# Sixteen copies of the residual spread over the first stage, and the biases and second expert's weights loaded after the first transposition

## The chip, the cores and the metric

The kernel runs on one core of a Trainium2 chip. The metric is the device time of one launch in microseconds (us), as the median of several runs. The core has a matrix engine (TensorE, PE in the profile), three engines for elementwise work (VectorE or DVE, ScalarE or ACT, GpSimd or POOL) and SyncE (SP), which here only issues DMA transfers. Each engine works its own list of instructions in order and waits on semaphores that others raise. The rows of SP's DMA issues stand under SPq.

## The reference

`x` is 128 x 64 x 256 in fp32, that is 8192 rows (tokens) of 256. A modulated linear layer makes a hidden row of each token, a mixture of eight experts is applied to it, and the result is added to `x`:

```python
scale = 1.0 / np.sqrt(np.float32(256)); ys = cond * scale                # per batch entry
d   = rsqrt(einsum('bi,io->bo', ys * ys, weight * weight) + EPS)
hid = einsum('bsi,io->bso', x * ys[:, None, :], weight) * d[:, None, :]
logits = hid @ wr.T; vals, idx = top_k(logits, 2); gating = softmax(only those two)
# each expert takes at most cap = 2560 tokens, in order of their number
xg = hid_pad[dispatch]                                                   # (8, cap, 256)
h  = gelu(einsum('ecd,edf->ecf', xg, w1) + b1[:, None, :])               # 256 -> 1024
y  = einsum('ecf,efd->ecd', h, w2) + b2[:, None, :]                      # 1024 -> 256
out = x + segment_sum(y * gate, dispatch)                                # back to the tokens
```

## The kernel before, in words

**First stage.** The tokens are worked in 16 groups (`GROUPS`) of 512. SP loads a group of the transposed `x` into one of four buffers (`load_x`, `X_RING` is 4), POOL scales it (line 336), PE multiplies it by the modulation weights (line 464), ACT and DVE scale the product (lines 672 and 810), PE turns it back to rows and computes the logits (lines 477 and 479), ACT copies the rows to `rows` (line 657). For every two groups (a set, `SETS` is 8) DVE picks the two best experts and a slot in their lists, POOL writes the gates, and SP stores the set in `hidden` in DRAM (`store_rows`, line 301). DVE and PE also build the lists of tokens; the one-hot matrices that this takes lie in the memory of `b2_sb` and `h_raw`, which is free for its own data only when all groups are listed (semaphore `listed`). The weights of the first expert are loaded at the start and split into a high and a low part during this stage (lines 648 and 779).

**Second stage.** Each expert's list is worked in blocks of 384 tokens. POOL gathers a block's rows from `hidden` with three indirect DMAs (`gather`, line 391), PE transposes them (line 537) and raises `t_done`, ACT makes the high part `xt_hi` (line 690), DVE the low part `xt_lo` (line 928). A block has eight chunks of 128 hidden units: `first_product` (lines 547 to 549), two GELU activations on ACT (line 701), a subtraction on DVE (line 969), `second_product` (lines 559 to 561). PE runs three first products ahead: the first product of chunk f waits for the GELU of chunk f-3 (`bank_read`). After the first product of chunk 6 PE transposes the rows of the next block. At the end of a block DVE adds `b2` (line 994) and multiplies by the gates, and POOL adds the rows into `out` in DRAM by an indirect DMA with addition (line 404). Before the first of these additions POOL waits for `out_written`, the count of the copies.

**Weights of the next expert.** `load_weights` is two DMAs of 1 MB each into `w_raw`. They may start when DVE has made all eight low parts of the expert before (`w_lo_done`). In the first two blocks of an expert, after the GELUs of chunks 2, 3, 4 and 5, ACT copies one piece of the next expert's weights each (`split_piece`, line 648), and DVE subtracts it (line 779). Before the first piece ACT waits for both DMAs (`w_loaded`), and its later GELUs stand behind this wait.

**Copies of x.** The output starts as a copy of `x`: `copy_x(g)` moves 512 KB from DRAM to DRAM in one DMA (line 280). Before the change SP issues the 16 copies in a row when everything is listed, behind the load of `b2`.

Of the kernel before, what the change touches and what calls it, by code (L numbers as in the profile page):

```python
# [16 lines left out]
P = 128  # L17
# [11 lines left out]
GROUPS = T // ROWS  # L29
GB = ROWS // S  # L30
PAIR = 2
SETS = GROUPS // PAIR
TS = PAIR * TILES
X_RING = 4
# [35 lines left out]
def build(nc, x, x_t, cond_t, w, wr_t, w1, b1_t, w2, b2, ident, tri, expert_low, slot_base, middle_ids, lanes,  # L70
# [9 lines left out]
    with ExitStack() as ctx:  # L80
        def sb(name, shape, dt=F32):
            return ctx.enter_context(nc.sbuf_tensor("sb_" + name, shape, dt))

        def sem(name):
            return ctx.enter_context(nc.semaphore(name))
# [16 lines left out]
        b2_sb = sb("b2", [P, E * D])  # L102
# [80 lines left out]
        b2_in = sem("b2_in")  # L183
# [32 lines left out]
        listed = sem("listed")  # L216
# [12 lines left out]
        t_done = sem("t_done")  # L229
# [37 lines left out]
        def all_blocks(eng, less=0):  # L267

            at = less * (E + 1) + E
            return eng.value_load(plan[0:1, at:at + 1], min_val=16 * (E * LEAST - less * LAG)) // 16  # L270
# [3 lines left out]
        @block.sync  # L274
        def _(sp):
            def load_x(g):
                sp.dma_start(x_in[g % X_RING][:, :, :], x_cols[g, :, :, :]).then_inc(x_loaded[g % X_RING], 16)

            def copy_x(g):
                sp.dma_start(out_copy[g, :, :], x_copy[g, :, :]).then_inc(out_written, 16)  # L280

            def load_weights(e):
                sp.dma_start(w_raw[:, 0:WCOLS].rearrange("p (k f) -> p k f", k=KC),
                             w1_rows[e, :, :, :]).then_inc(w_loaded, 16)
                sp.dma_start(w_raw[:, WCOLS:2 * WCOLS].rearrange("p (c d) -> p c d", c=FC),
                             w2_rows[e, :, :, :]).then_inc(w_loaded, 16)

            load_x(0)
            sp.dma_start(w_sb[:, :, :], w.rearrange("(k p) o -> p k o", p=P)).then_inc(w_in, 16)
            for g in range(1, X_RING):  # L290
                load_x(g)
            sp.wait_ge(set_dve, 1)
            for s in range(SUBS):
                sp.dma_start(hidden[T + s * P:T + (s + 1) * P, :], empty_sb[:, :]).then_inc(pad_zero, 16)
                sp.dma_start(out[T + s * P:T + (s + 1) * P, :], empty_sb[:, 0:D]).then_inc(out_written, 16)
            load_weights(0)

            def store_rows(s):

                sp.wait_ge(rows_ready, s + 1)  # L300
                sp.dma_start(hidden[s * TS * P:(s + 1) * TS * P, :].rearrange("(j p) c -> p j c", p=P),
                             rows[s % ROW_RING][:, :, :]).then_inc(rows_stored[s % ROW_RING], 16)

            for g in range(X_RING, GROUPS):
                sp.wait_ge(m_done, KC * (g - X_RING + 1))
                load_x(g)
                if g == X_RING + 2:
                    for tile, src in ((plan_sb[:, :], plan_consts), (b1_sb[:, :], b1_t),
                                      (slot_sb[:, :, :], slot_consts.rearrange("p (v t) -> p v t", v=3))):
                        sp.dma_start(tile, src).then_inc(late_in, 16)  # L310
                if g % 2 == 0 and g >= 8:
                    store_rows((g - 8) // 2)
            for s in range(GROUPS // 2 - 4, SETS):
                store_rows(s)
            sp.wait_ge(w_lo_done, PIECES)
            load_weights(1)
            sp.wait_ge(listed, GROUPS)
            sp.dma_start(b2_sb[:, :], b2.rearrange("e d -> (e d)").partition_broadcast(P)).then_inc(b2_in, 16)
            for g in range(GROUPS):
                copy_x(g)  # L320
            with sp.Fori(0, E - 2) as e:
                sp.wait_ge(w_lo_done, PIECES * (e + 2))
                load_weights(e + 2)
            sp.wait_ge(plan_ready, 1)
            n_all = all_blocks(sp)
            sp.wait_ge(added, n_all * (16 * SUBS))
            sp.sem_inc(sp_paced)

        @block.gpsimd
        def _(pool):  # L330
# [99 lines left out]
            pool.wait_ge(out_written, out_filled)  # L430
            pool.wait_ge(plan_ready, 1)
            _, end = plan_of(pool, 0)
            with pool.Fori(0, end - LAG) as b:
                next_block(b + LAG, (b + LAG) * SUBS)
# [13 lines left out]
        def _(pe):  # L448
# [164 lines left out]
            def expert(u, e, start, end):  # L613
# [4 lines left out]
                else:  # L618
                    one_block(u, 1 - u, end - 1, PIECES * (e + 2))

            _, end = plan_of(pe, 0)
            expert(0, 0, 0, end)
            with pe.Fori(0, E // 2 - 1) as pair:
# [8 lines left out]
        def _(act):  # L632
# [91 lines left out]
            bias(0, 0)  # L724
            act.wait_ge(plan_ready, 1)
            _, end = plan_of(act, 0)
            expert(0, 0, 0, end)
            with act.Fori(0, E // 2 - 1) as pair:
# [12 lines left out]
        def _(dve):  # L741
# [34 lines left out]
            def split_piece(u, i, count):  # L776
                cols = slice(i * PIECE, (i + 1) * PIECE)
                dve.wait_ge(w_hi_done, count)
                dve.tensor_tensor(w_lo[u][:, cols], w_raw[:, cols], w_hi[u][:, cols].bitcast(F32),
                                  ALU.subtract).then_inc(w_lo_done, 1)  # L780
# [143 lines left out]
            def split_rows(b):  # L924
                for k in range(KC):
                    rows_k = slice(k * SLOTS, (k + 1) * SLOTS)
                    dve.wait_ge(xt_hi_done, b * KC + (k + 1))
                    dve.tensor_tensor(xt_lo[:, rows_k], x_bank[k][:, 0:SLOTS], xt_hi[:, rows_k].bitcast(F32),  # L928
                                      ALU.subtract).then_inc(xt_ready, 1)

            def take_gates(b, first=False):

                if not first:
                    dve.wait_ge(y_ready, b * SUBS - SUBS)
                dve.wait_ge(gathered, b * (16 * SUBS) + 16 * SUBS)
                into = gates[:, bass.ds((b % 2) * (SUBS * E), SUBS * E)].rearrange("p (s e) -> p s e", e=E)
                dve.tensor_copy(into, xg[:, :, GATE_AT:GATE_AT + E]).then_inc(meta_done, 1)  # L937
# [28 lines left out]
            def split_chunk(b, f):  # L966

                dve.wait_ge(gelu_done, b * FC + (f + 1))
                dve.tensor_tensor(h_lo[f % RING][:, :], h_raw[f % RING],  # L969
                                  h_hi[f % RING][:, :].bitcast(F32), ALU.subtract).then_inc(h_ready, 1)  # L970

            dve.sem_inc(y_read, SUBS)
            dve.wait_ge(b2_in, 16)
            split_rows(0)
            take_gates(0, first=True)
            for f in range(2):
# [2 lines left out]
            def one_block(u, e, b, piece0, last=False):  # L979

                for f in range(2, FC):
                    split_chunk(b, f)
                    if f == 6 and not last:
                        split_rows(b + 1)
                        take_gates(b + 1, first=isinstance(b, int) and b == 0)
                    if piece0 is not None and f in SPLIT_AT:
                        i = piece0 + SPLIT_AT.index(f)
                        split_piece(1 - u, i, PIECES * (e + 1) + (i + 1))
                if not last:
                    split_chunk(b + 1, 0)  # L990
                for s in range(SUBS):
                    dve.wait_ge(y_free, b * SUBS + 1)
                    dve.wait_ge(y_done, b * SUBS + (s + 1))
                    dve.tensor_tensor(y[s][:, :], y_bank[s][:, 0:D], b2_sb[:, bass.ds(e * D, D)],  # L994
                                      ALU.add).then_inc(y_read, 1)
                if not last:
                    split_chunk(b + 1, 1)
                for s in range(SUBS):
                    dve.wait_ge(y_read, b * SUBS + (SUBS + s + 1))
                    dve.tensor_scalar(y[s][:, :], y[s][:, :], gates[:, bass.ds((b % 2) * (SUBS * E) + s * E + e, 1)],  # L1000
                                      None, ALU.mult).then_inc(y_ready, 1)

            def expert(u, e, start, end):
                for j in range(2):
                    one_block(u, e, start + j, j * len(SPLIT_AT))
                with dve.Fori(start + 2, end) as b:
                    one_block(u, e, b, None)
# [3 lines left out]
            with dve.Fori(0, E // 2 - 1) as pair:  # L1011
                for u in (1, 0):
                    e = pair * 2 + (2 - u)
# [3 lines left out]
            with dve.Fori(start, end - 1) as b:  # L1017
                one_block(1, E - 1, b, None)
# [48 lines left out]
```

## Time and profile before

| what | value |
|---|---|
| median of 3 runs | 1011.01 us (1010.73 to 1012.35) |
| the profiled execution's own time | 1011.03 us |
| its span | 1008.8 us |
| PE, ACT, DVE, POOL busy | 93%, 51%, 49%, 44% of the span |
| first stage, last matmul of the lists on PE ends | 158.8 us |
| first transposition of the second stage | at 175.94 us |
| SP: issue of the load of b2, first copy | at 158.85 us and 159.24 us |

The page cuts the span into 40 slices of 25.2 us and gives the busy tenths of each engine. Behind it stand views with times: the chain of work that ended last, the waits by engine, the issues of DMAs with the time until they landed, and the timeline.

### The profile page before, as it was taken

What the parts mean: (1) busy time and instruction counts of PE and PEld (TensorE: products, weight loads), DVE (VectorE), ACT (ScalarE), POOL (GpSimd) and SP (SyncE); (2) the same over time, 40 slices, a digit from 0 to 9 for tenths busy, and PEclk for the clock granted to TensorE, in tenths of its full rate; (3) what the DMA queues carried; (4) which work ended last, traced back from release to release, by engine and by line L of the source; (5) the groups of instructions that cost most, each with busy time, mean ns of one, the idle gap of its engine ahead of it and who ended that gap; (6) DMA issues with size and microseconds to landing.
All of it is one profiled execution on the core that took longest, in us unless ns stands there. A gap on an engine that the chain in (4) does not pass through costs nothing.

```text
span 1008.8 us, 19314 instructions
## 1 busy us (share of the span) xinstructions
PE 935.2 (93%) x6398; PEld 889.5 (88%) x6399; DVE 489.3 (49%) x1152; ACT 511.7 (51%) x1106; POOL 439.5 (44%) x480
## 2 busy tenths in 40 slices
PE   6887861999999999999999999999999999999994
PEld 3454540999999999999999999999999999999994
DVE  3678683453554346443544455345444544344441
ACT  3543330565565556555655556556455655545551
POOL 4142213253544545454454535445453544545433
PEclk9999985899999999999999999999999999999997
DMA  8434229552244323523252325323432232322322
GB/s 271 113 106 146 66 93 354 182 131 37 51 76 101 47 38 52 122 49 47 48 130 37 50 39 131 47 48 46 120 50 41 48 47 44 48 37 52 42 33 32
DMA packets 53466, 82.04 MB, mean 81 GB/s; under 512 B 6656, under 2 KB 42496, under 8 KB 53056
## 3 DMA queue, kind: packets, MB, share of 16 engines
q0 software_dynamic: 26496, 36.76, 23.3%
q1 hardware_dynamic: 25392, 44.42, 13.5%
q10 hardware_dynamic: 1552, 0.53, 0.2%
q8 instruction: 13, 0.21, 0.1%
q14 instruction: 13, 0.11, 0.0%
HBM read 54.16 MB, written 35.93 MB: 89 GB/s over the span
## 4 chain that ended last, share of the span: by engine, by line
PE 84%; DVE 9%; DMA 3%; issue 2%; POOL 1%; ACT 1%; SPq 0%; POOLq 0%; DVEq 0%
PE bank L559 13%; PE bank L560 13%; PE bank L561 13%; PE bank L548 13%; PE bank L547 13%; PE bank L549 13%; PE bank L537 3%; DMA sb_xg<-hidden,sb_gather_ids 2%; PE bank L464 1%; PE bank L477 1%; PE bank L479 1%; DVE sb_h_raw L890 1%; DVE sb_h_raw L876 1%; DVE sb_hid_t L810 1%; DVE sb_picked L860 1%
## 5 line engine op out<-in xcount | busy, mean ns | idle before, releaser
L969 DVE TENSOR_TENSOR sb_h_lo<-sb_h_raw,sb_h_hi 128x384 fp32r<-128x384 f32 x368 | 205.2, 558 | 321.5 <-ACT sb_h_hi L701 321.5
L701 ACT ACTIVATE sb_h_raw<-bank,sb_b_now 128x384 f32<-128x384 f32 x368 | 214.8, 584 | 282.2 <-PE bank L549 282.0
L559 PE MATMUL bank<-sb_w_hi,sb_h_hi 128*128 128x256 f32 x1104 | 315.1, 285 | 0.0
L560 PE MATMUL bank<-sb_w_lo,sb_h_hi 128*128 128x256 f32 x1104 | 311.6, 282 | 0.0
L561 PE MATMUL bank<-sb_w_hi,sb_h_lo 128*128 128x256 f32 x1104 | 310.1, 281 | 0.0
L404 POOL DMA_INDIRECT out_rows<-sb_y,sb_add_ids x138 | 222.8, 1614 | 67.8 <-POOL sb_add_ids L401 38.0
L547 PE MATMUL bank<-sb_xt_hi,sb_w_hi 128*128 128x384 f32 x736 | 250.0, 340 | 1.7 <-issue 1.7
L548 PE MATMUL bank<-sb_xt_lo,sb_w_hi 128*128 128x384 f32 x736 | 249.9, 340 | 0.0
L549 PE MATMUL bank<-sb_xt_hi,sb_w_lo 128*128 128x384 f32 x736 | 249.6, 339 | 0.0
L701 ACT ACTIVATE sb_h_hi<-bank,sb_b_now 128x384 fp32r<-128x384 f32 x368 | 212.3, 577 | 0.0
L561 PEld LDWEIGHTS bank<-sb_w_hi,sb_h_lo 128*128 128x128 f32 x1104 | 208.4, 189 | 0.0
L559 PEld LDWEIGHTS bank<-sb_w_hi,sb_h_hi 128*128 128x128 f32 x1104 | 208.0, 188 | 0.0
L560 PEld LDWEIGHTS bank<-sb_w_lo,sb_h_hi 128*128 128x128 f32 x1104 | 207.6, 188 | 0.0
L391 POOL DMA_INDIRECT sb_xg<-hidden,sb_gather_ids x138 | 136.8, 992 | 67.4 <-POOL sb_ids_ring L387 39.1
L547 PEld LDWEIGHTS bank<-sb_xt_hi,sb_w_hi 128*128 128x128 f32 x736 | 138.8, 189 | 2.1 <-issue 2.1
L548 PEld LDWEIGHTS bank<-sb_xt_lo,sb_w_hi 128*128 128x128 f32 x736 | 138.9, 189 | 0.0
L549 PEld LDWEIGHTS bank<-sb_xt_hi,sb_w_lo 128*128 128x128 f32 x736 | 138.9, 189 | 0.0
L386 POOL COPY sb_gather_ids<-sb_ids 128x3 int32 (+1 forms) x46 | 11.3, 247 | 265.6 <-DVE sb_gates L937 263.1
L690 ACT CAST sb_xt_hi<-bank 128x384 fp32r<-128x384 f32 x92 | 39.6, 483 | 111.3 <-PE bank L549 81.6
L928 DVE TENSOR_TENSOR sb_xt_lo<-bank,sb_xt_hi 128x384 fp32r<-128x384 f32 x92 | 47.1, 553 | 95.1 <-ACT sb_xt_hi L690 95.1
L994 DVE TENSOR_TENSOR sb_y<-bank,sb_b 128x256 f32<-128x256 f32 x138 | 50.1, 419 | 43.4 <-PE bank L561 43.4
L464 PE MATMUL bank<-sb_x,sb_w 128*128 128x512 f32 x128 | 63.8, 646 | 1.4 <-ACT sb_hid_t L672 1.4
(113 smaller groups left out, 622.0 us busy)
## 6 DMA issues: line engine op xcount, KB each, us to landing
sb_w_raw<-in_w SPq DMA_DIRECT2D x16, 1024.0 KB, 8.3
hidden<-sb_rows SPq DMA_DIRECT2D x8, 1056.0 KB, 6.3
sb_x<-in_x_t SPq DMA_DIRECT2D x16, 512.0 KB, 4.2
out_rows<-in_x SPq DMA_DIRECT2D x16, 512.0 KB, 14.1
sb_xg<-hidden,sb_gather_ids POOLq DMA_INDIRECT x138, 2.8
out_rows<-sb_y,sb_add_ids POOLq DMA_INDIRECT x138, 3.8
sb_b<-in_b SPq DMA_DIRECT2D x1, 1024.0 KB, 5.7
hidden<-sb_empty SPq DMA_DIRECT2D x3, 132.0 KB, 8.2
```

The costliest lines, as they stand in the source:

```text
L391: pool.indirect_dma_start(xg[:, s, :], None, hidden, bass.IndirectOffsetOnAxis(gather_ids[:, s:s + 1], axis=0),).then_inc(gathered, 16)
L404: pool.indirect_dma_start(out, bass.IndirectOffsetOnAxis(add_ids[:, s:s + 1], axis=0), y[s][:, :], None, compute_op=ALU.add,).then_inc(add ...
L464: mm = pe.matmul(m_bank[c % M_RING][:, :], w_sb[:, k, o * P:(o + 1) * P], x_in[g % X_RING][:, k, :], start=(k == 0), stop=(k == KC - 1))
L547: pe.matmul(h, w_hi[u][:, cols], xt_hi[:, rows], start=(k == 0), stop=False)
L548: pe.matmul(h, w_hi[u][:, cols], xt_lo[:, rows], start=False, stop=False)
L549: mm = pe.matmul(h, w_lo[u][:, cols], xt_hi[:, rows], start=False, stop=(k == KC - 1))
L559: pe.matmul(y, hi, w_hi[u][:, cols], start=(f == 0), stop=False)
L560: pe.matmul(y, hi, w_lo[u][:, cols], start=False, stop=False)
L561: mm = pe.matmul(y, lo, w_hi[u][:, cols], start=False, stop=(f == FC - 1))
L701: ins = act.activation(h, h_bank[f % H_BANKS][:, 0:SLOTS], ACT.Gelu_apprx_tanh, bias=b1_now[u][:, f:f + 1])
L969: dve.tensor_tensor(h_lo[f % RING][:, :], h_raw[f % RING], h_hi[f % RING][:, :].bitcast(F32), ALU.subtract).then_inc(h_ready, 1)
L994: dve.tensor_tensor(y[s][:, :], y_bank[s][:, 0:D], b2_sb[:, bass.ds(e * D, D)], ALU.add).then_inc(y_read, 1)
```

## The change

SP now issues one copy of `x` per group in the loop of the first stage, behind the load of `x` of that turn, and the last four behind the last four stores. It then waits until PE has transposed the first block, loads `b2`, and only after that the second expert's weights. DVE's wait for `b2` moves from ahead of the first block's `xt_lo` to ahead of the first addition of `b2`. No transfer and no arithmetic is added or removed.

```diff
                         sp.dma_start(tile, src).then_inc(late_in, 16)
+                copy_x(g - X_RING)
                 if g % 2 == 0 and g >= 8:
                     store_rows((g - 8) // 2)
             for s in range(GROUPS // 2 - 4, SETS):
                 store_rows(s)
+                copy_x(GROUPS - SETS + s)
+            sp.wait_ge(t_done, 1)
+            sp.dma_start(b2_sb[:, :], b2.rearrange("e d -> (e d)").partition_broadcast(P)).then_inc(b2_in, 16)
             sp.wait_ge(w_lo_done, PIECES)
             load_weights(1)
-            sp.wait_ge(listed, GROUPS)
-            sp.dma_start(b2_sb[:, :], b2.rearrange("e d -> (e d)").partition_broadcast(P)).then_inc(b2_in, 16)
-            for g in range(GROUPS):
-                copy_x(g)
...
             dve.sem_inc(y_read, SUBS)
-            dve.wait_ge(b2_in, 16)
             split_rows(0)
...
                     split_chunk(b + 1, 0)
+                if isinstance(b, int) and b == 0:
+                    dve.wait_ge(b2_in, 16)
                 for s in range(SUBS):
                     dve.wait_ge(y_free, b * SUBS + 1)
```

SP's list at the end of the first stage, in the kernel before. `hidden<-sb_rows` is the store of a set, `sb_w_raw` the weights, `sb_b<-in_b` is `b2`, `out_rows<-in_x` a copy:

```order
L277 DMA sb_x<-in_x_t 128x2x512
L301 DMA hidden<-sb_rows 128x8x264 x4
L283 DMA sb_w_raw<-in_w 128x2x1024
L285 DMA sb_w_raw<-in_w 128x8x256
L318 DMA sb_b<-in_b 128x2048
L280 DMA out_rows<-in_x 16x8192 x16
```

The same place in the changed kernel:

```order
L301 DMA hidden<-sb_rows 128x8x264
L280 DMA out_rows<-in_x 16x8192
L301 DMA hidden<-sb_rows 128x8x264
L280 DMA out_rows<-in_x 16x8192
L318 DMA sb_b<-in_b 128x2048
L283 DMA sb_w_raw<-in_w 128x2x1024
L285 DMA sb_w_raw<-in_w 128x8x256
```

The copies have moved ahead of the loads, one behind each store (and behind each load of `x` before), and `b2` now stands before the weights; all three loads stand behind a wait for the first transposition.

The first block's `xt_lo` on DVE, where only the place of the wait for `b2_in` moves (the lists show what each row waits for):

```order
-L928 TENSOR_TENSOR sb_xt_lo<-bank,sb_xt_hi 128x384 [waits xt_hi_done,b2_in]
-L928 TENSOR_TENSOR sb_xt_lo<-bank,sb_xt_hi 128x384 [waits xt_hi_done]
+L928 TENSOR_TENSOR sb_xt_lo<-bank,sb_xt_hi 128x384 [waits xt_hi_done] x2
```

And its list at the end of that block, the additions of `b2` (line 994, now 995):

```order
-L994 TENSOR_TENSOR sb_y<-bank,sb_b 128x256 [waits y_done,y_free] x3
-L969 TENSOR_TENSOR sb_h_lo<-sb_h_raw,sb_h_hi 128x384 [waits gelu_done]
-L1000 TENSOR_SCALAR sb_y<-sb_y,sb_gates 128x256 [waits y_read] x3
+L995 TENSOR_TENSOR sb_y<-bank,sb_b 128x256 [waits y_done,y_free,b2_in]
+L995 TENSOR_TENSOR sb_y<-bank,sb_b 128x256 [waits y_done,y_free] x2
```

The wait went from the block's first instruction on DVE to the first of the three additions at its end. On PE, ACT and POOL the order is what it was.

## Rows read from the trace of the kernel before

**Rows 1.** The page: busy tenths, clock and DMA share in 40 slices.
```profile
PE   6887861999999999999999999999999999999994
PEclk9999985899999999999999999999999999999997
DMA  8434229552244323523252325323432232322322
```
**Rows 2.** Three stretches: PE, PEld, DVE, ACT, POOL busy, PEclk, DMA share, GB/s.
```profile
100.00:150.00 50.00, 38.66 (x230) 25.77 (x229) 38.09 (x122) 19.83 (x70) 11.27 (x18) 0.91 0.23 77
150.00:176.00 26.00, 3.92 (x25) 2.50 (x23) 9.05 (x26) 0.00 (x0) 7.77 (x10) 0.50 1.02 347
193.00:1008.00 815.00, 801.63 (x5712) 799.80 (x5711) 367.75 (x825) 439.91 (x871) 385.27 (x404) 0.99 0.33 60
```
**Rows 3.** Chain that ended last, 163 to 192 us: start, us, what.
```profile
163.38 12.52 DMA sb_xg<-hidden,sb_gather_ids
...
175.94 1.55 PE bank L537 x6
177.52 0.49 ACT sb_xt_hi L690
178.10 1.02 DVE sb_xt_lo L928 x2
...
183.00 8.71 DMA sb_xg<-hidden,sb_gather_ids
191.75 0.88 PE bank L537 x6
```
**Rows 4.** SP's issues on the timeline: start, us, line, count.
```profile
30.23 6.28 SPq L277 DMA_DIRECT2D sb_x<-in_x_t  x2
...
36.56 0.47 SPq L301 DMA_DIRECT2D hidden<-sb_rows  x1
...
107.37 42.83 SPq L301 DMA_DIRECT2D hidden<-sb_rows  x4
150.25 1.80 SPq L283 DMA_DIRECT2D sb_w_raw<-in_w  x1
152.08 1.20 SPq L285 DMA_DIRECT2D sb_w_raw<-in_w  x1
158.85 0.34 SPq L318 DMA_DIRECT2D sb_b<-in_b  x1
159.24 10.59 SPq L280 DMA_DIRECT2D out_rows<-in_x  x16
```
**Rows 5.** The page: DMA issues by line, KB each, median us to landing.
```profile
sb_xg<-hidden,sb_gather_ids POOLq DMA_INDIRECT x138, 2.8
sb_b<-in_b SPq DMA_DIRECT2D x1, 1024.0 KB, 5.7
```
**Rows 6.** The same for issues at 149 to 150.2, 169 to 170 us.
```profile
hidden<-sb_rows SPq DMA_DIRECT2D x1, 1056.0 KB, 5.7
out_rows<-in_x SPq DMA_DIRECT2D x2, 512.0 KB, 21.3
```
**Rows 7.** Weights: issues at 210.06, at 210.56; all sixteen, min/median/max.
```profile
sb_w_raw<-in_w SPq DMA_DIRECT2D x1, 1024.0 KB, 6.8
sb_w_raw<-in_w SPq DMA_DIRECT2D x1, 1024.0 KB, 9.2
DMA to landing us min/median/max: 5.6/8.3/12.2
```
**Rows 8.** ACT in the first block, chunks 2 to 4.
```profile
185.24 0.62 ACT L648 CAST sb_w_hi<-sb_w_raw 128x512 fp32r<-128x512 f32 x1
185.74 0.59 ACT L701 ACTIVATE sb_h_raw<-bank,sb_b_now 128x384 f32<-128x384 f32 x1
186.22 0.59 ACT L701 ACTIVATE sb_h_hi<-bank,sb_b_now 128x384 fp32r<-128x384 f32 x1
```
**Rows 9.** PE: first and last matmul of chunk 6's first product.
```profile
190.47 0.34 PE L547 MATMUL bank<-sb_xt_hi,sb_w_hi 128*128 128x384 f32 x1
...
191.35 0.34 PE L549 MATMUL bank<-sb_xt_hi,sb_w_lo 128*128 128x384 f32 x1
```
**Rows 10.** POOL in the first stage: scaling of groups 7 and 8.
```profile
53.83 4.10 POOL L336 TENSOR_TENSOR sb_x<-sb_x,sb_ys_t 128x512 f32<-128x512 f32 x4
```
**Rows 11.** PE in the first stage: the same product before and after an idle time.
```profile
32.51 3.60 PE L464 MATMUL bank<-sb_x,sb_w 128*128 128x512 f32 x8
...
42.77 1.39 PE L511 MATMUL bank<-sb_b,sb_h_raw 128*128 128x168 f16 x8 [4.68 <-DVE sb_h_raw L890]
43.98 4.79 PE L464 MATMUL bank<-sb_x,sb_w 128*128 128x512 f32 x8
```

## The prediction

> **What bounds the kernel now.** I read the page's slices first. PE stands at 9 tenths from the eighth slice to the last but one and at 6 to 8 in the first stage; the one hole is the seventh slice (151 to 176 us), where PE is at 1, its clock at 5 and DMA at 9 tenths [rows 1]. The stretches say the same more sharply: from 150 to 176 us PE is busy 3.92 of 26 us, ACT not at all, and the DMA engines are full at 347 GB/s, while from 193 us on PE is busy 801.63 of 815 us [rows 2]. So what is saved or lost at the hole is carried to the end one for one: behind it PE is never free to catch up, and none of its work changes. The chain shows what the hole waits for: the last of the three gathers of the first block, issued at 163.38, landed 12.52 us later, and the transposition starts at 175.94 [rows 3]. The usual gather lands in 2.8 us, the median of 138 [rows 5]. What is in its way stands in SP's issues: the 16 copies, issued from 159.24 for 10.59 us [rows 4], the last of which land 21.3 us after their issue [rows 6]. The second block's gather meets the same copies, 8.71 us instead of 2.8, but this one costs PE only 0.2 us, from 191.53, when the matmul issued at 191.35 has had its turn (they follow each other every 0.18 us), to 191.75 [rows 3, 9].
>
> **What the change removes.** With the copies gone from the queue the gather should land in 2.8 us. The last set is stored at about 149.8 and lands in 5.7 us [rows 4, 6]; a last copy of 0.5 MB right behind it takes, at 347 GB/s [rows 2], 1.5 us more, so all is quiet by about 158, before the gathers begin. Nothing else late stands between: the weights of the second expert, which filled the queue from 150.25, are gone too. So the rows land at 163.38 + 2.8 = 166.2 instead of 175.9 and the second stage starts 9.7 us earlier (166.2 against 175.94). The 0.2 us of the second gather goes as well if that gather lands in time. Together 9.9 us is the most that can be had.
>
> **What it adds: a wait on ACT.** The weights of the second expert were issued at 150.25 and 152.08 [rows 4]; even with the longest landing of all, 12.2 us [rows 7], they were there at 164.3, and ACT used them at 185.24 without waiting [rows 8]. Now SP waits for the first transposition, which ends at 166.2 + 1.55 = 167.75 [rows 3], then issues b2 (0.34 us) and the two loads. 3.1 MB are under way from 167.8. The pair alone took 0.50 + 9.2 = 9.7 us from the first issue to the second landing [rows 7]; it starts at 168.2, so 177.9. In front of it stands b2, 1.05 MB: at 347 GB/s [rows 2] 3.0 us; as a whole transfer of its own 5.7 [rows 5]. Beside it runs the second block's gather, 384 rows of 1056 bytes, 0.4 MB, at most 1.2 us by the same rate. I take 177.9 + 3.0 + half of the 1.2 = 181.5 for the landing of the weights (W). Low end: b2 wholly beside the pair, 177.9. High end: the slowest landing, 0.50 + 12.2 = 12.7, and b2 at its full 5.7 and the gather at 1.2: 168.2 + 19.6 = 187.8.
>
> Who waits for W: ACT, in the first block, behind the GELU of chunk 2. With everything 9.74 us earlier ACT gets there at 185.24 - 9.74 = 175.5 and stands about 6 us. Behind it are the GELUs of chunks 3 to 7. PE needs the GELU of chunk 3 when it begins the first product of chunk 6, which was at 190.47 [rows 9] and would be at 180.73. From the start of the weight copy to the end of that GELU it is 186.22 + 0.59 - 185.24 = 1.57 us [rows 8], so PE can go on at W + 1.6 = 183.1, 2.4 us late. It is a single stop: afterwards ACT needs some 0.5 us for a piece and 1.0 for the two GELUs of a chunk, and PE over 2 us for a chunk, so ACT regains its lead. DVE stands in the same line behind ACT, but its subtraction is needed only after the product and the transposition. Net gain while W binds: 190.47 + 0.2 - (W + 1.6) = 189.1 - W, with W = 181.5 that is 7.6 us. Below W = 179.1 PE doesn't stop and the gain is 9.9; at the high end it is 1.3.
>
> **What I cost at nothing.** The copies in the first stage: DMA is busy 0.23 of the time from 100 to 150 us [rows 2]. Half a megabyte read and written takes some 1.7 us of a group's 9: the last copy, issued about 169.2, landed 21.3 us later at 190.5 [rows 6], the loads in front were done by about 164, and 26.5 / 16 = 1.7. The loads of x that they could hold up are early: the loads of groups 7 and 8 are issued from 30.23 [rows 4], and POOL scales these groups from 53.83 on [rows 10], about 17 us after the second. A store of a set is wanted by ACT only when its buffer comes round, four sets later. SP gives 0.6 us per issue out of idle time. Cover gone, the price would be the 10.59 us of issue time [rows 4]. Copy 0 stands behind the load of group 4, so the early and tight load isn't touched. The wait for b2 on DVE: b2 lands first of the three, by 167.8 + 5.7 = 173.5, and the addition comes some 25 us after the transposition. POOL's wait for the copies before its first addition was already over, and is earlier now. The half clock in which the first block starts (0.50 up to 176 us [rows 2]) stays: PE has been at half clock since before the hole. While W binds it doesn't matter, since W sets the time at which PE goes on.
>
> **A rule weighed.** The stretch with full DMA moved 347 GB/s [rows 2], and the pair with little beside it took 9.7 us for 2.1 MB [rows 7], 216 GB/s from issue to landing. The Trainium skill (DMA: Bandwidth & Descriptors, section Where 436 GB/s comes from) says that transfers between HBM and SBUF are held by HBM at about 358 GB/s per core. By that rate alone an estimate for 3.1 MB is 8.8 us, W would be 176.6, and rival B below would be the outcome. The trace gives the rate when the queue is full, but a short pair takes longer, so I stay with the rows.
>
> **Rivals.**
> B, no stop at all: the three loads overlap and land by 179.1. For it: the low end 177.9. Against: it leaves 1.2 us for b2 and gather, less than b2's 3.0. Gain 9.9, 1001.1 us.
> C, the second block's gather becomes the stop: it is issued at 183.00 - 9.74 = 173.3 amid the loads. If it took the 12.52 us of the first one now, it would land at 185.8 against 191.71, gain 5.9, 1005.1 us. Against: among copies it took 8.71, which is 182.0, in time while PE is at 184.2 for this transposition. The Trainium skill (the same page, section Queues, rings and completion order) says that a DMA engine goes round its queues packet by packet; small packets of weights would then hold a gather up less than those of a copy.
> D, the stop costs PE its clock: after 4.7 us without work (between 37.9 and 42.8) a product of eight took 4.79 us instead of 3.60 [rows 11]. A stop of 2.4 us with the same effect costs 1.2 more, up to twice that: gain 5.2 to 6.4, about 1005 us. Against: the stop is half as long.
> E, the gather is slow of itself and not by the copies. It is the first one, from rows just written. Then the second stage begins at 175.94 as before, the transposition ends at 177.5, W is 177.5 + 13.7 = 191.2, and 189.1 - 191.2 is a loss of 2.1 us, 1013.1; with the high end of W, 20 us after the transposition, it is 8.4, 1019.4. It decides from a landing of about 10.4 us for the gather. Against: the second gather, among the last copies, took 8.71, and all later ones 2.8.
> F, the copies slow the first stage: each group pays the issue or part of the transfer. From 0.48 us a copy the gain is gone; at the 0.66 us of an issue 10.6 are lost against 7.6 won, 1014.0. Against: the slack of 17 us above.
> That the change doesn't take the copies off the gather can't be: the last one is issued some 10 us before it.
>
> **How the numbers follow.** Forecast (W between 179.5 and 185): 54%; B 14%, C 10%, D 8%, E 7%, F 7%. The sum is made against the profiled 1011.03 us (span 1008.8 and 2.2 around it), which is the median of the runs, 1011.01, within 0.02. 1011.0 - 7.6 = 1003.4. The forecast's own range is 1001 to 1007; B and C are in a range of 1000.5 to 1008.5, and outside lie E, F and half of the high end. What can be told from no change is 0.2%, 2 us: faster 0.86 (all but E and F, and some of F small), same 0.07 (weights at the high end, mild E or F), slower 0.07.
>
> **What would show it.** The last gather of the first block lands in about 3 us and the transposition starts near 166; ACT's copy of the first piece of weights (line 648) has an idle time of about 6 us before it that ends with a DMA into sb_w_raw; PE has one stop of 2 to 3 us before the first product of chunk 6, and none before the transposition behind it; from 200 us on every event is about 8 us earlier; the end of the first stage stays at 159. The prediction is wrong if the first stage ends over 1 us later, if the gather takes over 5 us, or if PE's stop is over 5 us.

## The result, and the profile after

| | median | range | ratio to before, 95% interval |
|---|---|---|---|
| before | 1011.27 us | 1010.73 to 1012.35 (4 runs) | |
| changed | 1001.77 us | 1001.06 to 1002.82 (4 runs) | 0.9906 [0.9888, 0.9923] |
| changed, a second set | 1001.36 us | 1000.68 to 1002.04 (6 runs) | 0.9892 [0.9874, 0.9909] |

The change makes the kernel 9.5 us faster by the medians, 10.5 in the second set (beside 1011.87 us for the kernel before); 7.6 were forecast. One of the five runs of the kernel without copies (below) took 1863.34 us and is left out of its median and ratio. The profiled execution after has a span of 1000.9 us, 7.9 less than before. The page after, where the hole of [rows 1] was:

```profile
PE   6787873999999999999999999999999999999994
PEclk9998895999999999999999999999999999999998
DMA  9556344352343224432252325224432222322212
```

The seventh slice has gone from 1 to 3 on PE and from 9 to 4 on DMA, and the first six carry more DMA. The chain that ended last, against [rows 3] (start, us, what):

```profile
164.95 2.75 DMA sb_xg<-hidden,sb_gather_ids
167.70 0.04 issue
167.75 1.54 PE bank L537 x6
```

The last gather of the first block lands in 2.75 us instead of 12.52, and the transposition starts 8.2 us earlier (167.75 against 175.94). 9.8 us come from the gather; the gather itself is issued 1.57 us later than before (164.95 against 163.38), which is told below. On ACT, against [rows 8]:

```profile
177.02 0.57 ACT L701 ACTIVATE sb_h_hi<-bank,sb_b_now 128x384 fp32r<-128x384 f32 x1
181.01 0.62 ACT L648 CAST sb_w_hi<-sb_w_raw 128x512 fp32r<-128x512 f32 x1 [3.42 <-DMA sb_w_raw<-in_w]
181.54 0.58 ACT L701 ACTIVATE sb_h_raw<-bank,sb_b_now 128x384 f32<-128x384 f32 x1
182.01 0.57 ACT L701 ACTIVATE sb_h_hi<-bank,sb_b_now 128x384 fp32r<-128x384 f32 x1
```

The new wait is there: 3.42 us, ended by the DMA into `sb_w_raw`. PE at the first product of chunk 6, against [rows 9]:

```profile
182.62 0.28 PE L561 MATMUL bank<-sb_w_hi,sb_h_lo 128*128 128x256 f32 x1
182.74 0.35 PE L547 MATMUL bank<-sb_xt_hi,sb_w_hi 128*128 128x384 f32 x1
```

The line before it was issued 0.12 us earlier and there is no idle time: PE did not stop. Here it is 7.73 us ahead of the kernel before (190.47), at the next transposition 7.8 (183.95 against 191.75), and that stays to the end. Of the 8.19 us at the first transposition 0.46 are gone by then, though PE didn't wait: 13 of the first products' matmuls were 0.32 us apart, as at the half clock, where the kernel before had 10. Without this PE would have been at the product 0.46 us sooner and, with the weights landing when they did, would have stopped for some 0.3 us (an estimate), as it does in the second profile below.

SP's issues at the place show the loads behind the transposition:

```profile
151.83 0.59 SPq L280 DMA_DIRECT2D out_rows<-in_x  x1
169.32 0.34 SPq L318 DMA_DIRECT2D sb_b<-in_b  x1
169.71 0.43 SPq L283 DMA_DIRECT2D sb_w_raw<-in_w  x1
170.19 0.47 SPq L285 DMA_DIRECT2D sb_w_raw<-in_w  x1
```

and the list of DMA issues gives their landings, b2 first and then the two halves of the weights (KB, us from issue), which come out as 174.0, 176.9 and 181.0:

```profile
sb_b<-in_b SPq DMA_DIRECT2D x1, 1024.0 KB, 4.7
sb_w_raw<-in_w SPq DMA_DIRECT2D x1, 1024.0 KB, 7.2
sb_w_raw<-in_w SPq DMA_DIRECT2D x1, 1024.0 KB, 10.8
```

**Where 1.57 us went.** Up to 119.6 us the two first stages agree within 0.35 us. Then one product of eight takes longer. The chain before:

```profile
114.83 1.39 PE bank L511 x8
116.21 4.42 PE bank L464 x8
```

and after:

```profile
114.97 1.39 PE bank L511 x8
116.36 5.87 PE bank L464 x8
```

The stretches of 2 us show why. Before (PE, PEld, DVE, ACT, POOL busy, PEclk, DMA share, GB/s):

```profile
116.00:118.00 2.00, 2.00 (x5) 0.97 (x4) 1.83 (x8) 0.00 (x0) 0.00 (x0) 0.50 0.00 0
118.00:120.00 2.00, 2.00 (x5) 0.85 (x5) 1.53 (x8) 0.98 (x5) 0.00 (x0) 1.00 0.00 0
```

After:

```profile
116.00:118.00 2.00, 2.00 (x6) 0.94 (x5) 1.86 (x7) 0.00 (x0) 0.00 (x0) 0.50 0.00 0
118.00:120.00 2.00, 2.00 (x4) 0.94 (x3) 1.65 (x9) 0.06 (x1) 0.00 (x0) 0.50 0.00 0
120.00:122.00 2.00, 2.00 (x4) 0.63 (x3) 0.00 (x0) 1.68 (x8) 0.00 (x0) 0.73 0.00 0
```

TensorE was at 1.2 GHz (0.50) for longer after nearly the same idle time (3.58 us before, 3.60 after), with no DMA running in these stretches. Whether that is the copies' doing was the first question for the experiments.

### The profile page after: what moved, and what is told of

It is laid out like the page before. It is cut to its first block, busy times and chain, and to the rows that moved or that the text cites. A ratio compares the mean times of both kernels' runs of the same rounds, so it can differ in the third digit from the quotient of the medians.

```text
span 1000.9 us, 19313 instructions
## 1 busy us (share of the span) xinstructions
PE 936.9 (94%) x6398; PEld 890.7 (89%) x6399; DVE 489.0 (49%) x1152; ACT 511.4 (51%) x1106; POOL 439.2 (44%) x480
## 4 chain that ended last, share of the span: by engine, by line
PE 86%; DVE 8%; issue 2%; POOL 1%; DMA 1%; ACT 1%; SPq 0%; POOLq 0%; DVEq 0%
PE bank L559 13%; PE bank L560 13%; PE bank L561 13%; PE bank L547 13%; PE bank L548 13%; PE bank L549 13%; PE bank L537 3%; PE bank L464 2%; PE bank L477 1%; PE bank L479 1%; DVE sb_h_raw L890 1%; DVE sb_h_raw L876 1%; DVE sb_hid_t L810 1%; DVE sb_picked L860 1%; DVE sb_picked L859 1%
```

## The experiments

Ratios are to the kernel before, run on the same chip beside them. Ten kernels ran. Each line of a profile comes from one execution.

### No copies at all

The changed kernel with both `copy_x` lines taken out and `out_filled` lowered to `16 * SUBS`.

```diff
-                copy_x(g - X_RING)
...
-                copy_x(GROUPS - SETS + s)
```

> The changed kernel without any copy of x into the output; its output lacks the residual. Theory 1 (the 1.6 us by which the changed kernel's first stage ended later in its profile are a longer half-clock stretch of TensorE and no cost of the copies; the copies cost nothing where they stand): the same time as the changed kernel within 1 us, that is a ratio to the kernel before of 0.990 to 0.992; last gather of the first block lands in 2.7 us, weights wait on ACT of 3 to 4 us as in the changed kernel. Theory 2 (the copies slow the first stage by what the profile shows): 1.5 us faster than the changed kernel, ratio 0.988 to 0.989, and the last matmuls of the lists on PE start at 157.4 in every profile.

Measured: 1001.71 us, 0.9899 [0.9884, 0.9914]; the changed kernel has 0.9906 and 0.9892. So 8 MB of copies cost nothing that can be measured where they stand, and theory 1 holds. The last matmuls of the lists start at 157.63 here. PE does stop here, for 0.24 us:

```profile
181.12 0.44 PE L545 MATMUL bank<-sb_xt_hi,sb_w_hi 128*128 128x384 f32 x1 [0.24 <-ACT sb_h_hi L699]
```

### The changed kernel again

> The changed kernel itself again, beside the run above, for the comparison and to see its first stage a second time. If the longer half-clock stretch near 118 us of its first profile was chance, the last matmuls of the lists start between 157.4 and 159.0 us, and ACT's wait for the weights is again 3 to 4 us with PE stopping 0 to 0.5 us before the first product of chunk 6; if it belongs to the kernel, they start at 159.0. Ratio 0.989 to 0.992.

Measured: 1001.36 us, 0.9892 [0.9874, 0.9909], span of the profile 999.4. The last matmuls of the lists on PE:

```profile
157.63 1.39 PE L511 MATMUL bank<-sb_b,sb_h_raw 128*128 128x168 f16 x8 [1.59 <-DVE sb_h_raw L890]
...
166.34 1.54 PE L537 MATMUL bank<-sb_back,sb_xg 128*128 128x128 f32 x6 [7.32 <-DMA sb_xg<-hidden,sb_gather_ids]
...
181.15 0.44 PE L547 MATMUL bank<-sb_xt_hi,sb_w_hi 128*128 128x384 f32 x1 [0.29 <-ACT sb_h_hi L701]
```

The same program has its first stage 0.19 us later than before (157.63 against 157.44) and not 1.58: the longer stretch at half clock belongs to one execution and not to the kernel. Here the transposition comes 9.6 us earlier than before, chunk 6's product 9.3 and the end 9.4 (1008.8 - 999.4). This is the account that goes with the medians.

### Only the copies

The copies in the first stage; weights behind the last copy, `b2` behind `listed`, and DVE's wait as before.

```diff
-            sp.wait_ge(t_done, 1)
-            sp.dma_start(b2_sb[:, :], b2.rearrange("e d -> (e d)").partition_broadcast(P)).then_inc(b2_in, 16)
             sp.wait_ge(w_lo_done, PIECES)
             load_weights(1)
+            sp.wait_ge(listed, GROUPS)
+            sp.dma_start(b2_sb[:, :], b2.rearrange("e d -> (e d)").partition_broadcast(P)).then_inc(b2_in, 16)
```

> Only the copies move to the first stage; the second expert's weights are issued behind the last copy and b2 when all is listed, as before. Theory 1 (the copies alone held the first gather up; the waits that the moved loads add cost next to nothing): the first block's last gather lands in 3.5 to 6 us, since b2 and the end of the weights are still in the queue beside it, so the first transposition is 1 to 3 us later than in the changed kernel; ACT doesn't wait for weights; in all 0 to 3 us slower than the changed kernel, ratio 0.991 to 0.994. Theory 2 (the prediction as it was written: the wait for the weights costs 2.4 us in the changed kernel): it wins the 2.4 us back and is the same or up to 1.5 us faster than the changed kernel, ratio 0.989 to 0.991.

Measured: 1003.08 us, 0.991 [0.9896, 0.9925]. The gather, with b2 in the queue beside it, issued at 159.37:

```profile
163.88 2.87 DMA sb_xg<-hidden,sb_gather_ids
```

I had expected 3.5 to 6 us. The load of b2 overlaps the gathers; it landed 6.3 us after its issue, 1.8 us after the last gather was issued:

```profile
sb_b<-in_b SPq DMA_DIRECT2D x1, 1024.0 KB, 6.3
```

It doesn't hold them up. The moved copies alone give the gain (the span is 999.3 us, 999.4 in the changed kernel's second profile); what the moved loads add lies within the interval. The ratio stands where the two theories meet and doesn't choose between them.

### Only the loads

The copies in a row behind `listed`, as before, and `b2` and the weights behind the transposition.

```diff
-                copy_x(g - X_RING)
...
-                copy_x(GROUPS - SETS + s)
+            sp.wait_ge(listed, GROUPS)
+            for g in range(GROUPS):
+                copy_x(g)
             sp.wait_ge(t_done, 1)
```

> Only the loads move behind the first transposition; the 16 copies are issued in a row when all is listed, as before, and the loads stand behind them in the queue. Theory 1 (the order of the queue decides; the copies hold up what stands behind and beside them): the first gather lands in 9 to 12.5 us as before, the weights only after the last copy, at about 195 to 198 us, so that PE stops some 6 to 9 us in the first block: 1015 to 1020 us, ratio 1.005 to 1.009. Theory 2 (the weights of the second expert and b2 were what the gather waited for): the gather lands in under 6 us and the time is under 1008 us.

Measured: 1023.62 us, 1.011 [1.0095, 1.0126]: slower than either theory said. The chain at the first gather:

```profile
165.10 13.13 DMA sb_xg<-hidden,sb_gather_ids
```

PE at the first product of chunk 6:

```profile
201.78 0.69 PE L548 MATMUL bank<-sb_xt_hi,sb_w_hi 128*128 128x384 f32 x1 [9.05 <-ACT sb_h_hi L702]
```

The gather is slow with neither b2 nor weights beside it, so it was the copies. ACT gets the weights at 200.16, 2 us later than the latest that I had worked out, and PE stands for 9.05 us. I had left out that it goes on at half clock: 0.50 from 201.7 to 205. From this product to the end of the span it is 819.7 us, where the two profiles of the changed kernel have 818.2 and 818.3: 1.5 us more.

### The weights before the gather

The changed kernel with the second weights issued behind the last copy, ahead of the wait for the transposition.

```diff
-            sp.wait_ge(t_done, 1)
-            sp.dma_start(b2_sb[:, :], b2.rearrange("e d -> (e d)").partition_broadcast(P)).then_inc(b2_in, 16)
             sp.wait_ge(w_lo_done, PIECES)
             load_weights(1)
+            sp.wait_ge(t_done, 1)
+            sp.dma_start(b2_sb[:, :], b2.rearrange("e d -> (e d)").partition_broadcast(P)).then_inc(b2_in, 16)
```

> The changed kernel with one line moved: the second expert's weights are issued right behind the last store and copy, b2 stays behind the first transposition. Theory 1 (in the changed kernel the weights land just when PE needs the GELU behind them, so nothing is left to win there): the weights land by 163 to 165, partly beside the first gather, which takes 3 to 4 us; the same as the changed kernel within 1 us, ratio 0.989 to 0.992, with no wait of ACT for weights. Theory 2 (the wait costs PE 2.4 us): 2 to 2.5 us faster than the changed kernel, ratio 0.987 to 0.989.

Measured: 1001.89 us, 0.9897 [0.9882, 0.9913]; ACT doesn't wait for weights, the gather lands in 2.78 us. No difference from the changed kernel that the runs can tell, so the wait on ACT costs PE next to nothing.

### b2 three times: the same wait made longer

```diff
+            sp.wait_ge(b2_in, 16)
+            sp.dma_start(b2_sb[:, :], b2.rearrange("e d -> (e d)").partition_broadcast(P)).then_inc(b2_in, 16)
+            sp.wait_ge(b2_in, 32)
+            sp.dma_start(b2_sb[:, :], b2.rearrange("e d -> (e d)").partition_broadcast(P)).then_inc(b2_in, 16)
+            sp.wait_ge(b2_in, 48)
             sp.wait_ge(w_lo_done, PIECES)
...
-                    dve.wait_ge(b2_in, 16)
+                    dve.wait_ge(b2_in, 3 * 16)
```

> The changed kernel, but b2 is loaded three times, each load waiting for the one before, and only then the second expert's weights are issued. Theory 1 (ACT's wait for the weights is real and its cover in PE's lead is used up in the changed kernel): three loads of 4.5 us put the weights' landing 23 to 25 us behind the first transposition instead of 11.7, and PE stops 11 to 13 us before the first product of chunk 6, with some half clock behind: 1012 to 1016 us, ratio 1.000 to 1.005. Theory 2 (there is still cover of several us): the stop is under 9 us, ratio 0.993 to 0.998.

Measured: 1014.95 us, 1.0026 [1.0015, 1.0036]. ACT gets the weights at 192.48, 11.5 us later than in the changed kernel's profile, and PE stops for 10.91. ACT's first piece of weights:

```profile
192.48 0.62 ACT L653 CAST sb_w_hi<-sb_w_raw 128x512 fp32r<-128x512 f32 x1 [14.57 <-DMA sb_w_raw<-in_w]
```

The first product of chunk 6 on PE:

```profile
194.10 0.69 PE L552 MATMUL bank<-sb_xt_hi,sb_w_hi 128*128 128x384 f32 x1 [10.91 <-ACT sb_h_hi L706]
```

So the cover is used up in the changed kernel: weights that come 11.5 us later become 11.4 us at this product (194.10 against 182.74). The clock takes its share on top: the span is 13.9 us longer, so 2.5 us are lost behind this product (820.7 us from it to the end, against 818.2). The profiled execution is the slowest of the eight (1016.56 us); by the medians the kernel is some 12 to 13.5 us slower than the changed one. PE is at half clock behind the stop, in the stretches after it (columns as above):

```profile
194.00:197.00 3.00, 2.90 (x10) 2.81 (x11) 2.40 (x5) 3.00 (x8) 0.00 (x0) 0.50 0.00 0
197.00:200.00 3.00, 3.00 (x16) 3.00 (x15) 1.75 (x3) 1.43 (x3) 0.00 (x0) 0.53 0.02 5
200.00:205.00 5.00, 5.00 (x39) 5.00 (x38) 1.66 (x4) 2.77 (x6) 1.35 (x3) 1.00 0.00 0
```

This run also shows the pair of weights with nothing beside it, issued from 184.60:

```profile
sb_w_raw<-in_w SPq DMA_DIRECT2D x1, 1024.0 KB, 4.9
sb_w_raw<-in_w SPq DMA_DIRECT2D x1, 1024.0 KB, 7.4
```

From the first issue to the second landing that is 7.8 us (the second is issued at 185.02). The pair of [rows 7] took 9.7, but it wasn't alone. In the kernel before the queues moved this much from 210 to 220 us (packets, MB, share of the engines), SP's in the first line and the indirect transfers of POOL in the second:

```profile
q1 hardware_dynamic: 1312, 2.10, 62.3%
q0 software_dynamic: 239, 0.40, 21.2%
```

### The kernel before with its copies in runs of 4 KB

```diff
-    x_copy = x.rearrange("b s d -> (b s d)").rearrange("(g q r) -> g q r", g=GROUPS, q=16)
+    x_copy = x.rearrange("b s d -> (b s d)").rearrange("(g n q r) -> g q n r", g=GROUPS, n=8, q=16)
```

`out_copy` is changed alike, and `copy_x` takes one index more.

> The kernel before with one thing changed: each copy of x is described in runs of 4 KB (16 x 8 x 1024 elements) instead of runs of 32 KB, same bytes, same place behind b2. Theory 1 (a gather behind copies is slow because its small packets take turns with packets of 32 KB): the first gather lands in 4 to 8 us instead of 12.5 and the kernel takes 1004 to 1008 us, ratio 0.993 to 0.997. Theory 2 (it is the bytes in the queue and the full bandwidth): the gather lands in 11 to 13 us as before and the ratio is 0.998 to 1.002.

Measured: 1005.79 us, 0.9937 [0.9921, 0.9952]. The last gather, issued at 163.72, and the transposition behind it:

```profile
170.04 1.54 PE L537 MATMUL bank<-sb_back,sb_xg 128*128 128x128 f32 x6 [10.87 <-DMA sb_xg<-hidden,sb_gather_ids]
```

6.3 us instead of 12.5, with the same bytes in the same place; theory 1 holds. Up to the gather the copies are also issued at the same pace, one in some 0.65 us. Two thirds of what the change wins (0.63% of 0.94%) could be had by the shape of the copies alone.

### Filling PE's hole

56 matmuls that nobody reads, between the last list and the first transposition, in the changed kernel and in the one with the weights before the gather:

```diff
+            pe.wait_ge(row_copied, GROUPS * TILES)
+            for _ in range(56):
+                pe.matmul(bank[4][:, 0:P], ones_sb[:, :], tri_sb[:, :], start=True, stop=True)
             pe.wait_ge(gathered, 16 * SUBS)
```

> The changed kernel with 56 matmuls (128x128 by 128 columns, bf16, into a free bank, never read) on PE between the last list and the first transposition, so that PE works through the gather. Theory 1 (the half clock costs the first block about 2 us of PE time, but in the changed kernel the wait for the weights takes its place as soon as it is removed): the first products run at the full clock (0.34 us instead of 0.52 a matmul), PE then stops 1.5 to 2.5 us before the first product of chunk 6, and the time is that of the changed kernel within 0.5 us, ratio 0.990 to 0.992. Theory 2 (the wait for the weights has cover left): 1.5 to 2.5 us faster than the changed kernel, ratio 0.988 to 0.989. If the clock doesn't rise, no change either, and the matmuls' duration tells it.

> The same 56 matmuls in the kernel whose second weights are loaded before the gather (b2 behind the first transposition). Theory 1: no wait for the weights stands behind, so what the clock gives is kept: 1.5 to 2.5 us faster than the changed kernel, 999.5 to 1000.5, ratio 0.987 to 0.989. Theory 2 (the half clock at the start of the block is hidden anyway by ACT's and DVE's part of the first chunks): the same as without the matmuls, ratio 0.989 to 0.991.

Measured: 0.9914 [0.99, 0.9927] and 0.9901 [0.9886, 0.9916], neither different from the kernel it was made from. The first products still took 0.52 us a matmul in both, so they say nothing on what the half clock costs. The 56 end 2.2 to 2.5 us before the transposition. In the first, the weights landed late enough for a stop; from the product behind it to the end it is 818.2 us, as without a stop, so one of 1.5 us costs nothing more by the clock. ACT:

```profile
180.62 0.62 ACT L651 CAST sb_w_hi<-sb_w_raw 128x512 fp32r<-128x512 f32 x1 [5.16 <-DMA sb_w_raw<-in_w]
```

and PE:

```profile
182.24 0.44 PE L547 MATMUL bank<-sb_xt_hi,sb_w_hi 128*128 128x384 f32 x1 [1.50 <-ACT sb_h_hi L704]
```

The same with 82 of them, weights before the gather:

> The kernel with the second weights loaded before the gather, and 82 instead of 56 unread matmuls on PE, so that they reach up to about the first transposition instead of ending 2.2 us before it. Theory 1 (the 56 didn't raise the clock since PE still had a hole behind them; closed, the first products run at the full clock, and nothing else stands behind): first products of 0.34 us, 1.5 to 2 us faster than the changed kernel run beside it, ratio to the kernel before 0.987 to 0.989. Theory 2 (such matmuls don't count towards the clock here, or ACT and DVE hold the first chunks up): the first products stay at 0.52 us or PE waits for ACT instead; no difference within 0.5 us.

Measured: 1000.46 us, 0.9883 [0.9862, 0.9904], beside 0.9892 [0.9874, 0.9909] for the changed kernel: lowest of all medians, but the intervals overlap. PE's timeline shows that the clock rose and fell again:

```profile
166.48 0.88 PE L537 MATMUL bank<-sb_back,sb_xg 128*128 128x128 f32 x6 [1.08 <-DMA sb_xg<-hidden,sb_gather_ids]
169.03 0.41 PE L547 MATMUL bank<-sb_xt_hi,sb_w_hi 128*128 128x384 f32 x1 [1.67 <-issue]
169.28 0.45 PE L548 MATMUL bank<-sb_xt_lo,sb_w_hi 128*128 128x384 f32 x1
169.53 0.52 PE L549 MATMUL bank<-sb_xt_hi,sb_w_lo 128*128 128x384 f32 x1
```

The transposition ran at full clock (0.88 us against 1.54), the first products soon didn't. From the transposition to the first product of chunk 6 it is 13.69 us, against 14.50 in the kernel with early weights and no filling: 0.8 us in one profile each. The medians differ by 0.9 us, which the six runs of each don't tell from nothing, nor from twice as much. Neither theory is settled by it.

## Why the prediction was right, point by point

- **The copies hold the first gather up; without them it lands in 2.8 us.** Right: 2.75. Shown from both sides: the copies moved alone give the gain, and the loads moved alone leave the gather at 13.13 us. Rival E (slow of itself) falls.
- **What is won at the hole reaches the end.** Right: 9.3 us at the product of chunk 6, 9.4 at the end in the second profile.
- **ACT waits for the weights, about 6 us, and PE goes on at W + 1.6.** The mechanism is right, and the 1.6 exact wherever PE stopped: 179.50 and 181.12 without copies, 180.62 and 182.24 with the 56 matmuls, 192.48 and 194.10 with b2 three times, 200.16 and 201.78 with the loads alone, 1.62 each time. The wait itself is shorter than forecast, 3.42 us, and 3.95 in the second profile.
- **PE stops for 2.4 us.** This is the mis-sized term: it was 0 and 0.29 us. I had put W 13.75 us behind the end of the transposition (181.5 - 167.75); it was 181.01 - 169.29 = 11.7. The 2 us too many lie in what I added to the pair of weights, 3.0 us for b2 and 0.6 for the gather. The second half of the weights landed 10.8 us after its issue against 9.2 in [rows 7], so that 1.6 were to be added and not 3.6. I had read the pair of [rows 7] as almost alone, but POOL moved 0.40 MB beside it, as much as the gather here (0.41 MB): the 0.6 was counted twice, and b2 cost 1.6 instead of 3.0. With b2 three times the pair was alone and took 7.8 us; above that b2 and the gather together did cost 3.5. These are single loads; the second halves of the eight pairs before landed in 8.1 to 12.2 us. Why b2 in front costs the pair half of its 3.0 us isn't shown by a run of its own. The DMA engines weren't full in the 9.7 us (250 GB/s from 210 to 220 us), and from 169.3 to 181.1 they moved 3.55 MB at 301 GB/s, which agrees with transfers that fill each other's gaps, but is argued and not tested. The outcome lies between the forecast (W at least 11.75 us behind the transposition) and rival B (at most 11.35), at B's border. The Trainium skill's rate (DMA: Bandwidth & Descriptors, section Where 436 GB/s comes from) gave an estimate of 8.8 us for the three loads; the measured 11.7, which hold the time from the first issue to the last landing, are 2.9 above it and 2.0 below mine.
- **Rival C (the second gather).** Didn't come about: PE has no idle time before the second transposition, at 183.95 in the first profile.
- **Rival D (the clock behind a stop).** Not in the changed kernel, since there is no stop worth it; it is real behind long stops: from the first product of chunk 6 to the end it takes 818.2 us behind a stop of 0 or 1.50 us, 819.7 behind one of 9.05 and 820.7 behind one of 10.91, so that the clock costs nothing, 1.5 and 2.5 us.
- **Rival F (a slower first stage).** Its sign was in the first profile, 1.57 us, and I might have booked it as the copies' price. Without any copy the time is the same, and a second profile of the same program has 0.19. The kernel with the loads alone, which has no copy in the first stage, is 1.74 us late there (159.18): four matmuls at 17.60 us took 3.62 us where the kernel before needs 1.98.
- **What the sum lacked.** 9.5 measured against 7.6, inside my range of 1001 to 1007 us but at its low end: the 2.4 us of the stop less the 0.3 that was there is that difference, within 0.2. The first profile's 7.9 agrees with the forecast by accident: two longer stretches at half clock, of 1.4 us near 118 us and of 0.46 at the start of the block, in place of the stop.

## What to carry to other kernels

Bulk copies that nobody waits for belong in a stage whose DMA engines are mostly idle; issued in a row just before a small gather on the critical path they made it land in 12.5 us instead of 2.8. Where they can't be moved, try them in shorter runs: here that won two thirds as much. When a load is moved behind an event to clear the queue, find the engine that waits for it, what is queued behind that wait, and how far the engine it feeds runs ahead: here three chunks of lead covered a wait of 4 us to within 0.3, and nothing beyond it.

## What the hardware showed that I had not expected

- The size of the runs of a copy has a large part in how long a gather on another queue takes beside it: 12.5 us beside runs of 32 KB, 6.3 beside runs of 4 KB, 2.87 beside the load of b2 (8 KB a partition), 2.75 alone. The rule of the Trainium skill (DMA: Bandwidth & Descriptors, section Queues, rings and completion order), that an engine switches between queues only at packet borders, agrees with the first two; I had used it against rival C only and not seen that it offered a remedy. That the gather beside b2 is hardly slower isn't explained by run size alone; b2 is 1 MB where the copies are 8, and it had landed 1.1 us before the last gather did; no run tells the two reasons apart.
- The same program can have its half-clock stretch near 116 us 1.4 us longer in one execution than in another, with nearly the same idle time before it (3.58 us before, 3.60 after). In nine of the twelve profiles the last matmuls of the lists start at 157.4 to 158.0 us, in the other three at 159.0 to 159.5. A difference of 1.5 us between two single profiles of this kernel is not yet a finding.
